# A graph layer on one Trainium2 core: the first row blocks' adjacency stage interleaved with the first normalisation pass

## The reference

```python
h = relu(layernorm(x))                       # x: 4096 x 256
e = (h @ edge_w) @ (h @ edge_w).T            # 4096 x 4096 scores
e = where(adj > 0, e, NEG_BIG)               # adj: 4096 x 4096, about one in 1024 is 1
out = adj * (softmax(h @ node_w, axis=0) * softmax(e, axis=1)) @ (h @ weight)
x = x + out + bias
h = relu(layernorm(x))
x = x + hyperbolic_layer(h, adj, W1)         # a second sum over the neighbours
```

## Time and profile before

| | us |
|---|---|
| median of 3 runs | 1017.33 |
| lowest, highest | 1014.04, 1020.45 |
| span of the profiled execution (first to last instruction) | 819.8 |
| what lies around the span, against the median | 197.5 |
| first front (to the end of its last ACT copy) | 0 to 77.0 |
| first step of the edge pipeline (adjacency stage of group 0) | 77.2 to 105.5 |
| second step | 105.5 to 134.1 |
| whole edge pipeline, to its last reduction | 77.2 to 471 |

### The profile page before, as it was taken

The page is one execution under the profiler, slowest core; times in us unless marked ns, Lnnn a source line. Parts: engine busy times, 40 slices in busy tenths (PEclk is TensorE's granted clock), DMA queues, the critical chain, the costliest instruction groups (busy, mean ns, idle before and its releaser), DMA issues.

```text
span 819.8 us, 13067 instructions
## 1 busy us (share of the span) xinstructions
PE 512.1 (62%) x3644; PEld 422.6 (52%) x3644; DVE 456.8 (56%) x1839; ACT 343.8 (42%) x719; POOL 388.2 (47%) x447
## 2 busy tenths in 40 slices
PE   3766463768786869797787758800475566656600
PEld 2555242657676668686777736700354445544500
DVE  3674368778774787778925277551133333333256
ACT  2466753555555456463230357760112111121157
POOL 4246027475765635555573000001777777777600
PEclk9799856969898898889988968965668877787765
DMA  8541979969787487772231000033444444444306
GB/s 326 169 138 48 405 281 340 328 234 348 236 302 270 146 314 240 270 276 81 74 101 53 1 2 1 1 119 100 102 106 105 106 106 104 101 104 104 94 0 205
DMA packets 43911, 131.99 MB, mean 161 GB/s; under 512 B 7120, under 2 KB 24400, under 8 KB 35664
## 3 DMA queue, kind: packets, MB, share of 16 engines
q1 hardware_dynamic: 27344, 84.88, 27.9%
q0 software_dynamic: 16512, 46.49, 21.3%
HBM read 118.69 MB, written 12.65 MB: 160 GB/s over the span
## 4 chain that ended last, share of the span: by engine, by line
PE 29%; issue 20%; DVE 18%; ACT 11%; POOL 7%; DMA 5%; DVEq 5%; POOLq 3%; ACTq 2%; SPq 0%; PEldq 0%
PE bank L1231 9%; PE bank L680 6%; POOL work L1178 5%; PE bank L224 4%; PE bank L637 3%; ACT work L520 3%; DMA work<-in_adj 3%; POOLq L131 3%; ACT work L1244 2%; PE bank L729 2%; DVE gx L1611 2%; ACT front L197 2%; DVE fs L893 2%; POOL work L586 2%; DVEq L1024 1%
## 5 line engine op out<-in xcount | busy, mean ns | idle before, releaser
L586 POOL DMA_INDIRECT work<-table_h,work x160 | 163.8, 1024 | 103.4 <-issue 73.5
L1178 POOL DMA_INDIRECT work<-table_y,work x160 | 156.6, 979 | 50.0 <-issue 48.8
L1231 PE MATMUL bank<-work 128*128 128x257 f32 x320 | 116.2, 533 | 81.8 <-issue 47.9
L1231 PEld LDWEIGHTS bank<-work 128*128 128x128 f32 x320 | 83.2, 270 | 104.0 <-issue 49.7
L520 ACT ACTIVATE work<-work 128x2048 bf16<-128x2048 f32 x64 | 121.7, 1901 | 36.1 <-PE bank L637 28.3
L680 PE MATMUL bank<-work 128*128 128x128 f32 x640 | 100.5, 322 | 19.2 <-DVEq L939 19.2
L680 PEld LDWEIGHTS bank<-work 128*128 128x128 f32 x640 | 94.2, 233 | 20.7 <-DVEq L939 17.5
L1248 ACT ACTIVATE work<-bank 128x257 f32 x32 | 12.3, 385 | 165.8 <-PE bank L1231 165.8
L637 PE MATMUL bank<-work 128*128 128x256 bf16 x512 | 73.5, 298 | 11.5 <-ACT work L520 11.5
L1195 DVE TENSOR_SCALAR work<-work 128x640 bf16<-128x640 f16 x32 | 14.0, 436 | 117.1 <-PE bank L1225 116.7
L637 PEld LDWEIGHTS bank<-work 128*128 128x128 bf16 x512 | 52.3, 106 | 27.4 <-ACT work L520 16.6
(11 more groups left out here) (239 smaller groups left out, 950.1 us busy)
## 6 DMA issues: line engine op xcount, KB each, us to landing
work<-in_adj SPq DMA_DIRECT2D x64, 1024.0 KB, 7.1
table_y<-work SPq DMA_DIRECT2D x8, 520.0 KB, 6.4
front<-in_x SPq DMA_DIRECT2D x8, 512.0 KB, 4.5
table_h<-front SPq DMA_DIRECT2D x8, 512.0 KB, 3.2
front<-in_x POOLq DMA_DIRECT2D x8, 512.0 KB, 4.9
out<-gx SPq DMA_DIRECT2D x8, 512.0 KB, 3.0
work<-table_h,work POOLq DMA_INDIRECT x160, 5.5
work<-table_y,work POOLq DMA_INDIRECT x160, 2.8
```

The lines of the kernel that those rows point to most:

```text
L586: p.indirect_dma_start(gat[:, k, n, :], None, table_h, bass.IndirectOffsetOnAxis(ix[:, k, n:n + 1], 0)) \
L1178: p.indirect_dma_start(gt2[:, k, n, :], None, table_y, bass.IndirectOffsetOnAxis(ix2[:, k, n:n + 1], 0)) \
L1231: last = t.matmul(bank[4 + b % 2][:, 0:DY], otf[:, b % 2, q, :], gt2[:, k, b * TILES + q, 0:DY], start=(q == 0), stop=(q == TILES - 1))
```

## The change

The adjacency stage of group 0 (eight units) is done within the first front. At each front step n from 3 to 10, behind the front's own work of that step, ACT converts unit n-3, and PE packs unit n-3. DVE takes the keys of blocks 0 and 1 behind its step 6, and those of blocks 2 and 3 and the edge list behind step 10. ACT also converts units 0 and 1 of group 1 behind step 10. SP issues the halves of blocks 2 to 5 between its front stores and loads, from step 2's store onwards, and its later loop begins at block 6. The packed words of the early stage lie in banks 6 and 7, since the front uses 0 to 5. The front's loop is written out on all engines but POOL. The `key` buffer moves from the front's memory to `fs`. The edge pipeline's own loop starts at step 1. DVE's reduction of the logits, which gives `s_red`, stays behind the front, and so comes behind the edge list.

```diff
-        def staged(eng, body):
+        def staged(eng, body, begun=0, rolled=True, beside=None):
             def step(n):
                 stage = lambda d: (n - d, (n - d) % 2) if 0 <= n - d < NG else None
                 body(stage(0), stage(1), stage(2), stage(3))
+                if beside:
+                    beside(n)
+            if not rolled:
+                for n in range(begun, NG + 3):
+                    step(n)
+                return
+            for n in range(begun, 3):
...
-        key = spare[:, 0:2 * KEY].rearrange("p (a b) -> p a b", a=2)
+        key = fs[:, 0:2, :]
...
+        def load_block(e, n, k, halves=range(UNITS)):
+            for h in halves:
+                if isinstance(n, int) and n < 2:
...
+                else:
+                    e.wait_ge(L["conv"], UNITS * (n - 2) + h + 1)
+                    e.dma_start(adu[:, k, h, :], adj[bass.ds(n * P, P), h * UW:(h + 1) * UW]).then_inc(L["adj"][k][h], 16)
+        EARLY = GB + 2
+        def early_half(e, v):
+            n = 2 + v // UNITS
+            load_block(e, n, n % 2, (v % UNITS,))
...
+        def early_act(a):
+            def beside(n):
+                if n >= 3:
+                    unit_conv(a, 0, 0, n - 3)
+                if n == NG + 2:
+                    unit_conv(a, 1, 1, 0)
+                    unit_conv(a, 1, 1, 1)
+            return beside
...
-                for u in range(2 if ls else 0, UNITS * GB):
+                for u in range(2, UNITS * GB):
                     conv(u, wd)
...
+        def early_pe(t):
+            t.wait_ge(s_const, 1)
+            t.sem_inc(L["pack"], UNITS)
+            def beside(n):
+                if n >= 3:
+                    unit_pack(t, 0, n - 3, (6, 7))
+            return beside
...
+        def early_dve(d):
+            d.sem_inc(L["key"], 2)
+            def beside(n):
+                if n == 6:
+                    keys(d, 0, 0, 0, (6, 7))
+                if n == NG + 2:
+                    keys(d, 0, 0, 1, (6, 7))
+                    edge_list(d, 0, 0, None)
+            return beside
...
-            with e.Fori(0, (NG - 2) // 2) as j:
-                for k in (0, 1):
-                    store(2 * j + k, k)
-                    load(2 * j + k + 2, k)
-            store(NG - 2, 0)
-            store(NG - 1, 1)
+            for g in range(NG):
+                store(g, g % 2)
+                if g + 2 < NG:
+                    load(g + 2, g % 2)
+                if g >= 2:
+                    early_half(e, g - 2)
+            for v in range(NG - 2, UNITS * (EARLY - 2)):
+                early_half(e, v)
             fast_load(e)
...
-            staged(a, first)
+            staged(a, first, rolled=False, beside=early_act(a))
...
-            staged(t, front_pe(f0, rhs_g, DY))
+            staged(t, front_pe(f0, rhs_g, DY), rolled=False, beside=early_pe(t))
...
-            staged(d, first)
+            staged(d, first, rolled=False, beside=early_dve(d))
```

More of the change, by code:

```diff
@@ L139, in step @@
                 body(stage(0), stage(1), stage(2), stage(3))
-            for n in range(3):
+                if beside:
[5 more added lines that the diff above has]
+            for n in range(begun, 3):
                 step(n)
@@ L497, in fast_constants, with unit_conv @@
                             channel_multiplier=-1)
-            p.drain()
+            p.drain().then_inc(s_const, 1)
+        def load_block(e, n, k, halves=range(UNITS)):
+            for h in halves:
+                if isinstance(n, int) and n < 2:
+                    e.dma_start(adu[:, k, h, :], adj[n * P:(n + 1) * P, h * UW:(h + 1) * UW]).then_inc(L["adj"][k][h], 16)
+                else:
[5 more added lines that the diff above has]
+            load_block(e, n, n % 2, (v % UNITS,))
         def fast_load(e):
-            with e.Fori(0, (NB - 2) // 2) as j:
+            with e.Fori(0, (NB - EARLY) // 2) as j:
                 for n in range(2):
[L503 to L506, removed]
+                    load_block(e, 2 * j + EARLY + n, n)
+        def unit_conv(a, g, k, u):
+            b, h = u // UNITS, u % UNITS
+            a.wait_ge(L["adj"][b % 2][h], 16 * (2 * g + b // 2 + 1))
+            a.wait_ge(L["pack"], UNITS * GB * g + UNITS * b + h + 1)
+            a.activation(abf[:, h, :], adu[:, b % 2, h, :], ACT.Copy,
+                         accum_out=cnt[:, k, b, h:h + 1]).then_inc(L["conv"], 1)
+        def early_act(a):
[6 more added lines that the diff above has]
+            return beside
         def fast_act(a):
@@ L619, in gnn_program, with unit_pack @@
         EB = (3, 4, 5)
+        def unit_pack(t, g, u, banks):
+            b, h = u // UNITS, u % UNITS
+            into = bank[banks[b % 2]]
+            if h == 0:
+                t.wait_ge(L["key"], GB * g + b + 1)
+                t.matmul(into[:, 0:KEY], idb, iokb, start=True, stop=False)
+            t.wait_ge(L["conv"], UNITS * GB * g + UNITS * b + h + 1)
+            for m in range(BITS // UNITS):
+                mm = h * BITS // UNITS + m
+                last = t.matmul(into[:, 0:KEY], wid[:, mm, :], abf[:, h, m * KEY:(m + 1) * KEY],
+                                start=False, stop=(mm == BITS - 1))
+            last.then_inc(L["pack"], 1)
+        def early_pe(t):
[5 more added lines that the diff above has]
+            return beside
         def fast_pe(t):
-            t.sem_inc(L["pack"], UNITS)
             t.sem_inc(L["agg"], 2 * GB)
@@ L628, in pack @@
                     if wd:
[L629 to L639, removed]
+                        unit_pack(t, wd[0], u, (0, 1))
                 def proj(b):
@@ L767, in body, with keys, edge_list @@
                     last.then_inc(L["mx"], 1)
[L768 to L792, removed]
+            staged(t, body, 1)
+        def keys(d, g, k, pair, banks):
+            bs = (2 * pair, 2 * pair + 1)
+            d.wait_ge(L["pack"], UNITS * GB * g + UNITS * (2 * pair + 2) + UNITS)
+            d.tensor_copy(ddum[:, :], eps_t[:, :])
+            for b in bs:
+                d.max(t16[:, k, b, 0:8], bank[banks[b % 2]][:, 0:KEY])
+            d.drain()
+            for b in bs:
+                d.match_replace(key[:, b % 2, :], t16[:, k, b, 0:8], bank[banks[b % 2]][:, 0:KEY], -1.0) \
+                    .then_inc(L["key"], 1)
+            d.drain()
+            for b in bs:
+                d.max(t16[:, k, b, 8:16], key[:, b % 2, :])
+            d.drain()
+        es_sums = bank[2][:, 0:GB * SLOTS].rearrange("p (b s) -> p b s", s=SLOTS)
+        def early_dve(d):
[7 more added lines that the diff above has]
+            return beside
+        def edge_list(d, g, k, at_):
                 ti, tw = ia.bitcast(I32), ib.bitcast(I32)
@@ L846, in edge_list, with fast_dve @@
                 d.drain()
+        def fast_dve(d):
+            d.memset(zeros, 0.0)
+            d.drain()
+            d.sem_inc(L["otp"], 1)
+            d.sem_inc(L["x1"], 2 * GB)
+            bc = lambda v, shape, axis: v.unsqueeze(axis).broadcast_to(shape)
             def edges(g, k):
@@ L969, in body @@
                 if wd:
-                    keys(*wd, 0)
+                    keys(d, *wd, 0, (0, 1))
                 if at_:
@@ L974, in body @@
                 if wd:
-                    keys(*wd, 1)
+                    keys(d, *wd, 1, (0, 1))
                 if wd:
-                    edge_list(*wd, at_)
+                    edge_list(d, *wd, at_)
                 elif at_:
@@ L1331, in _ @@
             e.dma_start(bias_bc[:, :], bias.rearrange("(a d) -> a d", a=1).broadcast_to([P, D])).then_inc(s_w2, 16)
-            for n in range(2):
-                for h in range(UNITS):
-                    e.dma_start(adu[:, n, h, :], adj[n * P:(n + 1) * P, h * UW:(h + 1) * UW]).then_inc(L["adj"][n][h], 16)
+            load_block(e, 0, 0)
+            load_block(e, 1, 1)
             def store(g, k):
```

15 lines of the change are left out of this document (6 added, 9 removed).

## The result

The changed kernel takes 1036.38 us (median of 4 runs, 1035.35 to 1036.93), the kernel before, run beside it, 1016.55 us (4 runs, 1014.04 to 1020.45). The ratio is 1.0169 with a 95% interval of 1.0123 to 1.0216: 19.8 us slower, by the interval somewhere from 12.5 to 22. The forecast was 1034.

A forecast was written before the change was run, and what follows sets the result against it. The front step was taken as a latency-bound loop PE, ACT, DVE, PE of 6.97 us, lengthened to 11.1 by the pack's wait; the seam came 17 us later, so 1017.3 + 17 = 1034 us, range 1024 to 1043.

The forecast's parts named there:

- The loop and the wait: First front: PE waits at the pack for ACT's conversion, 4.2 us idle; steps take 11.1 us against 6.97.
- Hidden after all: Front: PE's transposes get ahead of the pack; line 952 comes 9.6 us earlier, total time 1008 us; chance 6%.
- The products: PE's product starts in the front: step 4 at 36.4 us, step 8 at 82.8, step 9 at 93.5, step 10 at 102.5.
- The step of 13.1 with the keys: Front step up to step 8's product: 11.1 us and 2.0 more, for DVE's keys of blocks 0 and 1.
- the transposes: PE's transposes in each front step: 1.03 us at the full clock, 1.5 taken at the lower, 1.3 in the sum.
- The written-out loops: Written-out front loops: more instructions to fetch, costing between nothing and 1 us.
- The choice between 10.0 and 12.2 us a step: PE's clock in the front: 10.0 us a step at the full clock, 12.2 at the lower; mean 11.1 taken.
- The counts: Counts' matmul on PE at the seam, behind keys and edge list: at 120.5 us in place of 105.47, 15 later.
- The load of the library: POOL's reduction library at the seam: 11.4 us from POOL's last subtraction, running beside the edge list, ready at 122.2 us.
- rival 4: Seam: POOL loads its library behind the wait for `s_red`; 27 us later, total time 1044 us; chance 4%.
- that 197.5 us lie around the span: Whole kernel: 197.5 us of the 1017.33 median lie outside the profiled 819.8 us span, untouched by the edit.
- all is as before, only later: Behind the seam: everything unchanged but later; the pipeline's second step stays 28.6 us long, give or take 2.

The follow-up runs named there:

- The kernel that does this by its order: The change with PE packing each unit one front step after ACT converted it; 813.19, 809.46 us on quick chips, 995.86 on a slow one (ratios 0.986, 0.9782, 0.9967).
- the filled kernel: The change with twenty extra unused matmuls on PE ahead of each early pack; 838.65 us, ratio 1.0122 to the kernel before, beside the change's 839.95.
- the kernel that loads it twice: The kernel with the pack one step later, plus an early POOL reduction of a constant and `s_red` ahead of the last keys; 999.97 us (980.27 to 1007.89).

## Why the prediction was right

**The loop and the wait.** That PE would stand at the pack, and the transposes and the product behind it, is shown three ways: by the rows (idle of 3.7 to 5.1 us ended by L531), by taking the wait away (products 6.4 to 8.7 us apart, the front back to 75), and by doubling what is waited for (17.8 us for eight conversions).

**The rival on the other side.** Hidden after all was put at 9.6 us faster, if PE's transposes got ahead of the pack. The kernel that does this by its order is 14 and 18 us faster than the kernel before on quick chips, and 3 (0 to 7) on a slow one. So the direction was right and the size lies between these, and that nothing in the change's streams lets PE get ahead was right too.

**The terms.** The products were forecast at 36.4, three steps of 11.1, 82.8, 93.5 and 102.5; they are at 37.65, then 11.9, 11.3 and 11.3 apart, 85.22, 96.02 and 104.69. The step of 13.1 with the keys took 13.0. Mis-sized were the transposes: 1.5 us was taken at the lower clock, between 1.03 and twice that, and they take 1.91 or 1.92, near the upper end, in each of the steps 4 to 9. The sum had 1.3 for them, between the two clocks; from their start to the product's it is 1.7 in each of these steps (59.20 to 60.90). That is 0.4 us six times; with the 0.9 us by which this profile's step 3 started later (22.27 against 21.40) it is more than the 2.2 us by which step 10's product missed its forecast, and the other terms came out a little short. The written-out loops were put at a cost of nothing to 1 us, more instructions to fetch; alone they made the kernel 6 us faster. That term had the wrong sign, and what they gain outside the front is open.

**The clock.** The choice between 10.0 and 12.2 us a step, by the granted clock, was the largest uncertainty of the sum. The mean was 0.79 over the front's long steps, and the packs ran at both speeds (1.89, 1.79, 1.89, 1.18, 1.89, 1.12, 1.20, 1.05 us for the eight). It was shown as a cause in the front by the filled kernel: ordinary steps of 10 to 11 us, step 10's product 5.2 us earlier, 4.3 without the head start of 0.9. By the rule of the Trainium skill ("TensorE: Matmul & The Clock Gate", "What's actually happening"), an idle stretch brings the throttle back. The trace agrees: PE is idle 4.0 to 6.4 us ahead of the four packs that ran at the lower speed, and 3.1 to 3.7 ahead of the four that did not. Even behind two of these the transposes ran at a granted clock of 0.50 (70.52 to 72.23 is one).

**The seam.** The counts were forecast at 120.5, the reduction at 122.2 and DVE's start at 122.9; they are 123.37, 125.08 and 125.53, each 2.6 to 2.9 later. The front's 2.2 is carried on, and the last pack starts 8.5 us behind step 10's product (113.15 less 104.69) where 7.6 was taken. The load of the library runs ahead of the wait, as line 601 in the earlier trace rows had said: MODIFY_POOL_CONFIG at 114.5, long before the logits are reduced (123.84). In all nine profiles of kernels with this order (the change three times, and its variants) the reduction comes 0.8 to 1.9 us behind the counts' matmul, not 11. So rival 4 is ruled out. Which of the two ends last is a matter of about a microsecond: DVE's reduction of the logits in seven of the nine, the load in the first profile of the change and in the first of the pack one step later. The Trainium skill ("GPSIMD Engine Reference", "2.1 Instruction dispatch") puts such a load at about 6 us. That lies under what is seen here: with nothing else to wait for, 11.0 us in the earlier trace rows, 10.6 after, 9.7 in the kernel that loads it twice, and 6.8 at that kernel's first load (10.6 to 17.4); only that one is near it.

**The total.** 17 us were forecast behind the seam; 19.6 are there in the profile of the change and 19.8 in the runs. The step that was wrong stands at the beginning and was harmless: that 197.5 us lie around the span. They lie inside it, on slow chips. The waits show it (engine, tile, line, what was waited for; us in total, times, longest); in the profile of the change, from 150 to 600 us:

```profile
POOL work L617 <- PE bank L722: 121.7, 6, 23.3
ACT front L571 <- PE bank L722: 118.8, 27, 25.4
ACT work L531 <- remote: 78.9, 8, 13.6
```

and on a quick chip, from 150 to 500 us:

```profile
ACT front L571 <- PE bank L722: 117.3, 32, 17.9
POOL work L617 <- issue: 61.2, 143, 3.2
...
ACT work L531 <- PE bank L661: 23.6, 12, 2.9
```

There ACT waits 79 us, in eight pieces, for something outside the engines that the profile does not name ("remote"); here it waits for PE, in pieces under 3 us. The transfers themselves are not slower by their packets. The pages of the kernel before (first profile, span 819.8) and of the change (span 1034.6) have in their queues, with packets, MB and the time of the packets as a share of the span:

```profile
q1 hardware_dynamic: 27344, 84.88, 27.9%
q0 software_dynamic: 16512, 46.49, 21.3%
...
q1 hardware_dynamic: 27344, 84.88, 23.1%
q0 software_dynamic: 16512, 46.49, 16.7%
```

That is 229 and 175 us of packets' time before, and 239 and 173 after. So what the slow chips wait for is open. The sum worked all the same because a delay at the seam is added to either pipeline. That it is passed on whole was argued from "all is as before, only later"; the runs show it only roughly: 19.8 us (12.5 to 22) of 19.6 on the first slow chip, 12.8 (10.8 to 16.6) of 17.2 on a quick one. The mechanism at the seam was right; that the run's shift came so near to the forecast 17 on the first chip is in part luck.

## What to carry to other kernels

Work that is put beside a latency-bound loop must fit every engine's order, not only every engine's idle time. Before placing a consumer, ask what stands behind it in its own stream; here a pack of 1 us, placed one step too early, held up the loop by 4, and placing it a step later turned 1.7% of loss into a gain of 1.4 and 2.2% on quick chips (0.3% on a slow one, not clear of none). A short wait on PE can cost twice in its own stage, as the work behind it may run at the lower clock; here that did not reach the end of the run.

## What was not expected of the hardware

- One and the same kernel takes 827 us on two of the chips, 998 on a third, and 1017 where the result was measured. The front is alike on both kinds. The second step of the edge pipeline takes 41 to 42 us on slow chips and 27 to 30 on quick ones, a later one 49 to 61 and 35 to 51. The packets are the same in number, bytes and, nearly, time.
- A gain at the seam of 31 us (pack later against the change) is 18 at the last group's counts on a slow chip, and 30 (92.63 against 123.03) is 29 on a quick one. Why the slow one takes up so much is open: no profile of the kernel before was made there.
- Transposes of eight 128 x 128 tiles in f32 take 1.92 us at the lower clock, against 1.03 at the full one: nearly the factor of two between the clocks.
- The library of the reduction is loaded again at 82.3 us although it had been loaded at 10.5 and used at 17.4. Between them POOL had changed back for its subtractions, which held it up as well: 7.8 us idle ahead of the one at 39.9.
